# A four-layer graph network on one core: the norm ahead of the graph convolutions, done chunk by chunk in the gated-update stage, with its scaling and its split piece by piece under the first convolution

## The reference

```
h = relu((x - mean(x)) / sqrt(var(x) + 1e-5))
messages = segment_sum(h[src] @ W_msg.T + b_msg + edge_embed[type], dst)
x = x + gru_cell(messages, h, W_ih, W_hh, b_ih, b_hh)      # the gated update

h = relu((x - mean(x)) / sqrt(var(x) + 1e-5))              # the norm of this case
for k in 1, 2, 3:                                          # three graph convolutions
    h = D^-1/2 (A + I) D^-1/2 (h @ W_k.T) + b_k            # relu after the first two
x = x + h
```

## Time and profile before

| | |
|---|---|
| median of 3 runs | 6476.04 us (6473.61 to 6477.31) |
| the profiled execution, its own time | 6473.09 us |
| its span in the profile | 6471.3 us |
| TensorE busy | 4680.4 us (72%) |
| VectorE busy | 2656.4 us (41%) |
| ScalarE busy | 1449.9 us (22%) |
| GpSimd busy | 3123.8 us (48%) |
| gated-update stage | about 4600 to 5118 us of the span |
| norm block and split block | about 5120 to 5174 us |
| first, second and third convolution | begin at about 5175, 5605 and 6035 us |

### The profile page before, as it was taken

The page is one execution under the profiler, slowest core; times in us unless marked ns, Lnnn a source line. Parts: engine busy times, 40 slices in busy tenths (PEclk is TensorE's granted clock), DMA queues, the critical chain, the costliest instruction groups (busy, mean ns, idle before and its releaser), DMA issues. The chain is left out here.

```text
span 6471.3 us, 90519 instructions
## 1 busy us (share of the span) xinstructions
PE 4680.4 (72%) x25880; PEld 3137.8 (48%) x25881; DVE 2656.4 (41%) x5995; ACT 1449.9 (22%) x2542; POOL 3123.8 (48%) x3318
## 2 busy tenths in 40 slices
PE   1755555555555538888888888889599599899898
PEld 0444444444444435555555555556244344444444
DVE  4666666666666644444444444442311400000000
ACT  2111111111111123333333333331211201111000
POOL 3177777777777737777777777772000000000000
PEclk5855555555555568888888888886799799999999
DMA  3432233323323324444444444441444165555555
GB/s 98 170 93 92 93 92 93 93 92 93 93 93 93 94 79 131 134 133 132 132 131 130 130 130 130 130 130 41 140 155 158 39 218 193 168 193 193 170 193 155
DMA packets 337459, 817.56 MB, mean 126 GB/s; under 512 B 126730, under 2 KB 147748, under 8 KB 321174
## 3 DMA queue, kind: packets, MB, share of 16 engines
q1 hardware_dynamic: 218110, 516.64, 23.8%
q0 software_dynamic: 105568, 215.74, 12.2%
q10 hardware_dynamic: 13696, 84.07, 3.5%
HBM read 700.32 MB, written 114.23 MB: 126 GB/s over the span
## 5 line engine op out<-in xcount | busy, mean ns | idle before, releaser
L852 POOL DMA_INDIRECT e_rows<-scratch_table,e_staged x1616 | 1524.6, 943 | 658.1 <-issue 492.2
L1267 POOL DMA_INDIRECT e_rows<-scratch_table,e_staged x1616 | 1537.2, 951 | 587.6 <-issue 485.2
L171 PE MATMUL e_win<-e_onehot,e_rows 128*128 128x64 f32 x3232 | 783.0, 424 | 987.7 <-DMA e_rows<-scratch_table,e_staged 966.8
L171 PEld LDWEIGHTS e_win<-e_onehot,e_rows 128*128 128x128 f32 x3232 | 720.2, 328 | 1057.3 <-issue 1027.3
L1565 PE MATMUL c_sums<-ring,parts 128*128 128x512 bf16 (+1 forms) x3822 | 790.1, 368 | 80.9 <-DMA c_bias<-in_conv_b 80.9
L1375 DVE TENSOR_TENSOR e_z<-e_p,e_rows 128x512 f32<-128x512 f32 x404 | 279.3, 691 | 1155.1 <-PE e_p L1318 956.6
L1789 POOL DMA_DIRECT2D c_w<-in_convT x3 | 1.6, 535 | 1442.5 <-POOLq L77 1442.5
L1565 PEld LDWEIGHTS c_sums<-ring,parts 128*128 128x128 bf16 x3822 | 361.8, 98 | 490.1 <-DMA c_bias<-in_conv_b 81.5
L171 PEld LDWEIGHTS e_win<-e_onehot,e_msg 128*128 128x128 f32 x3232 | 477.2, 212 | 247.8 <-issue 218.0
L1298 PE MATMUL e_p<-h,we 64*128 64x512 f32 x808 | 282.8, 782 | 364.0 <-DMA h<-in_edge_T 359.9
L208 DVE TENSOR_SCALAR e_onehot<-e_iota,dst_rel,weight 128x64 f32<-128x64 f32 x1616 | 443.2, 336 | 244.7 <-issue 244.1
(11 more groups left out here) (236 smaller groups left out, 4792.2 us busy)
## 6 DMA issues: line engine op xcount, KB each, us to landing
ring<-scratch_counts SPq DMA_DIRECT2D x336, 896.0 KB, 4.7
h<-in_time_rows SPq DMA_DIRECT2D x101, 1024.0 KB
e_rows<-scratch_table,e_staged POOLq DMA_INDIRECT x3232
h<-in_edge_T SPq DMA_DIRECT2D x101, 512.0 KB, 4.2
scratch_counts<-h ACTq DMA_DIRECT2D x12, 3136.0 KB, 10.4
scratch_counts<-type_mem ACTq DMA_DIRECT2D x12, 3136.0 KB, 10.4
scratch_table<-table_tile SPq DMA_DIRECT2D x49, 512.0 KB, 2.6
ring<-scratch_counts SPq DMA_DIRECT2D x28, 224.0 KB, 2.9
```

The lines of the kernel that those rows point to most:

```text
L171: last = nc.tensor.matmul(win[:, 0:W], rows[:, j, :], onehot[:, j, :], start=(j == 0), stop=(j == J - 1))
L852: pool.indirect_dma_start(rows[:, half * NB + b, j, :], None, A["table0"], bass.IndirectOffsetOnAxis(ap=staged[:, half, b * J + j:b * J + ...
L1267: pool.indirect_dma_start(rows[:, half * NB + b, j, :], None, A["table1"], bass.IndirectOffsetOnAxis(ap=staged[:, half, b * J + j:b * J + ...
```

## The change

In the gated-update stage each chunk gets four more instructions, made right after its `x` is done. VectorE (`center`) sums the rows of the chunk, writes `x - sum/128` into `h` in one instruction, and, after ScalarE has squared it into `square`, sums the squares. ScalarE makes that square between the wait for `x` and the copy to `agg`. The block of the norm and the block of the split are gone. What is left of both now stands in the first convolution's block: `norm_pieces` on VectorE, behind its wait for weights and bias, and `split_pieces` on ScalarE. They make the variance, root, reciprocal and product with `dinv` once, and then, piece by piece, relu with scaling in one instruction, and the three parts. In product(0) of the first convolution TensorE waits for the third part of each piece before it uses it. The gated-update stage has 4 semaphores more, and each of the three convolution blocks has 7 more.

```diff
@@ -1552,7 +1552,7 @@
             pe.sem_inc(s["d_used"], 1)
             return load_flag(pe, s, pe.alloc_register(f"flag_pe_{s['used'].name}"))
 
-        def product(pe, s, above, loaded, ring, digit_ring, parts, sums, c, k, tiles, self_loops):
+        def product(pe, s, above, loaded, ring, digit_ring, parts, sums, c, k, tiles, self_loops, ready=None):
 
             width = tiles * P
 
@@ -1569,6 +1569,8 @@
             pe.wait_ge(s["out"], c + 1)
             for j in range(PIECES):
                 pe.wait_ge(loaded[j], c * 16 + 16)
+                if ready is not None:
+                    pe.wait_ge(ready, j + 1)
                 if j == PIECES - 1:
                     with pe.If(above > 0):
                         with pe.Fori(1, PLANES) as plane:
@@ -1617,7 +1619,7 @@
                 pN = psum(st, "p3N", [P, 2, BANK])
                 s = {n: sem(st, f"n3_{n}") for n in
                      ("used", "out", "w", "bias", "MT", "mh", "gates", "biased", "rz_in", "rz", "pre", "new", "v", "x", "held",
-                      "begun", "d_used", "d_loaded")}
+                      "begun", "d_used", "d_loaded", "summed", "centered", "squared", "ssq")}
                 loaded = [sem(st, f"n3_loaded{j}") for j in range(PIECES)]
                 st.callback(clear_semaphores)
                 block = st.enter_context(nc.Block())
@@ -1689,6 +1691,9 @@
                             act.wait_ge(s["pre"], u + 1)
                             nc.scalar.activation(new[:, 0:before, :], pre[:, 0:before, :], ACT.Tanh).then_inc(s["new"], 1)
                             act.wait_ge(s["x"], u + 1)
+                            act.wait_ge(s["centered"], u + 1)
+                            nc.scalar.activation(square[:, 0, 0:before, :], h[:, bass.ds(u * 4, before), :],
+                                                 ACT.Square).then_inc(s["squared"], 1)
                         if tiles:
                             act.wait_ge(s["used"], c * PIECES + 2 * PIECES)
                             nc.scalar.activation(agg[:, k, 0:tiles * P], sums[:, k, 0:tiles * P],
@@ -1708,6 +1713,19 @@
                         if tiles:
                             nc.vector.tensor_copy(held[:, k, 0:tiles, :],
                                                   h[:, bass.ds(c * 4, tiles), :]).then_inc(s["held"], 1)
+                        if before:
+                            center(c - 1, before)
+
+                    def center(u, before):
+
+                        at = bass.ds(u * 4, before)
+                        dve.wait_ge(s["x"], u + 1)
+                        nc.vector.tensor_reduce(mean[:, at], x[:, at, :], AXX, ALU.add).then_inc(s["summed"], 1)
+                        dve.wait_ge(s["summed"], u + 1)
+                        nc.vector.scalar_tensor_tensor(h[:, at, :], mean[:, at].unsqueeze(2).to_broadcast([P, before, D]),
+                                                       -1.0 / D, x[:, at, :], ALU.mult, ALU.add).then_inc(s["centered"], 1)
+                        dve.wait_ge(s["squared"], u + 1)
+                        nc.vector.tensor_reduce(ssq[:, at], square[:, 0, 0:before, :], AXX, ALU.add).then_inc(s["ssq"], 1)
 
                     def gru(u, before):
                         dve.wait_ge(s["gates"], u + 1)
@@ -1741,27 +1759,10 @@
                     run_chunks(step)(dve)
 
 
-        with ExitStack() as st:
-            s = norm_sems(st, "n4")
-            st.callback(clear_semaphores)
-            block = st.enter_context(nc.Block())
-
-            @block.vector
-            def _(dve):
-                norm_vector(dve, s, h, extra_scale=dinv)
-
-            @block.scalar
-            def _(act):
-                norm_scalar(act, s, h)
-                act.wait_ge(s["h"], PIECES)
-
-
-
         h_b = h[:, :, :].rearrange("p t d -> p (t d)").bitcast(BF16)
         parts = [[sbuf(root, f"parts3{k}", [P, NT, D], BF16)[:, :, :] for k in range(3)],
                  [v.rearrange("p (t d) -> p t d", d=D) for v in
                   (h_b[:, 0:NP], h_b[:, NP:2 * NP], type_mem[:, :].bitcast(BF16)[:, 0:NP])]]
-        split_all("split3", parts[0])
         for conv in range(3):
             last_conv = conv == 2
             with ExitStack() as st:
@@ -1779,6 +1780,11 @@
                      ("used", "out", "O", "y", "h", "part", "rest", "x", "begun",
                       "d_used", "d_loaded")}
                 loaded = [sem(st, f"c{conv}_loaded{j}") for j in range(PIECES)]
+                first_conv = conv == 0
+                s_part = [sem(st, f"c{conv}_part{k}") for k in range(3)]
+                s_gap, s_norm = [sem(st, f"c{conv}_gap{k}") for k in (1, 2)], sem(st, f"c{conv}_norm")
+                s_h0 = sem(st, f"c{conv}_h0")
+                piece_gap = sbuf(st, "piece_gap", [P, 3, PT, D]) if first_conv else None
                 s_store = sem(st, f"c{conv}_store")
                 w_base = weights_seen(32)
                 st.callback(clear_semaphores)
@@ -1807,7 +1813,8 @@
 
                     def step(c, k, tiles, before):
                         if tiles:
-                            product(pe, s, above, loaded, ring, digit_ring, now, sums, c, k, tiles, True)
+                            product(pe, s, above, loaded, ring, digit_ring, now, sums, c, k, tiles, True,
+                                    s_part[2] if first_conv and not before else None)
                         if before:
                             pe.wait_ge(s["out"], c + 2)
 
@@ -1821,6 +1828,21 @@
                 @block.scalar
                 def _(act):
                     act.sem_inc(s["out"], 2)
+
+                    def split_pieces():
+                        act.wait_ge(s_norm, 1)
+                        nc.scalar.activation(std[:, :], var[:, :], ACT.Sqrt).then_inc(s_norm, 1)
+                        for j in range(PIECES + 2):
+                            if j < PIECES:
+                                act.wait_ge(s_h0, j + 1)
+                                nc.scalar.activation(now[0][:, piece(j), :], h[:, piece(j), :], ACT.Copy).then_inc(s_part[0], 1)
+                            for k in (1, 2):
+                                if 0 <= j - k < PIECES:
+                                    act.wait_ge(s_gap[k - 1], j - k + 1)
+                                    nc.scalar.activation(now[k][:, piece(j - k), :], piece_gap[:, (j - k) % 3, :, :],
+                                                         ACT.Copy).then_inc(s_part[k], 1)
+                    if first_conv:
+                        split_pieces()
 
                     def step(c, k, tiles, before):
                         if before:
@@ -1843,6 +1865,32 @@
                 @block.vector
                 def _(dve):
                     dve.wait_ge(weights_in[0], w_base + 32)
+
+                    def norm_pieces():
+
+                        nc.vector.tensor_scalar(var[:, :], ssq[:, :], 1.0 / D, EPS, ALU.mult, ALU.add).then_inc(s_norm, 1)
+                        dve.wait_ge(s_norm, 2)
+                        nc.vector.reciprocal(rstd[:, :], std[:, :]).then_inc(s_norm, 1)
+                        dve.wait_ge(s_norm, 3)
+                        nc.vector.tensor_tensor(rstd[:, :], rstd[:, :], dinv[:, :], ALU.mult).then_inc(s_norm, 1)
+                        dve.wait_ge(s_norm, 4)
+                        for j in range(PIECES + 2):
+                            if j < PIECES:
+                                nc.vector.scalar_tensor_tensor(h[:, piece(j), :], h[:, piece(j), :], 0.0,
+                                                               rstd[:, piece(j)].unsqueeze(2).to_broadcast([P, PT, D]),
+                                                               ALU.max, ALU.mult).then_inc(s_h0, 1)
+                            if 0 <= j - 2:
+                                g = piece_gap[:, (j - 2) % 3, :, :]
+                                dve.wait_ge(s_part[1], j - 1)
+                                nc.vector.tensor_tensor(g, g, now[1][:, piece(j - 2), :], ALU.subtract).then_inc(s_gap[1], 1)
+                            if 0 <= j - 1 < PIECES:
+                                dve.wait_ge(s_part[0], j)
+                                if j >= 4:
+                                    dve.wait_ge(s_part[2], j - 3)
+                                nc.vector.tensor_tensor(piece_gap[:, (j - 1) % 3, :, :], h[:, piece(j - 1), :],
+                                                        now[0][:, piece(j - 1), :], ALU.subtract).then_inc(s_gap[0], 1)
+                    if first_conv:
+                        norm_pieces()
 
                     def step(c, k, tiles, before):
                         if not before:
```

## The result

The changed kernel takes 6443.64 us, median of 5 runs (6437.60 to 6447.53), against 6476.04 us before (6473.61 to 6478.91). The ratio is 0.9948, with a 95% interval of 0.9934 to 0.9963: faster by 0.5%, 32.4 us by the medians, where 38.0 were forecast. The forecast was 6438 with a range of 6433 to 6448. The profiled execution took 6444.22 us; its span is 6442.4, and before it was 6471.3, so that the two profiles stand 28.9 apart.

The account below looks back on a forecast made before the run. It took TensorE's 65.20 us without a matmul before the first convolution as the bound. New terms sum to 25.81, 37.98 less with 1.41 for semaphores: 6435.1, plus 2.95 to the median, 6438.1; own range 6434 to 6445, whole 6433 to 6448.

Parts of the forecast that it names:

- step of chunk 12, wait: Gated update: the short 8.37 us product gives no cover, so `agg` of chunk 11 makes TensorE 2.25 us late.
- last step, wait: Gated update's last step: the same delay of `agg`, with a `held` of one tile, adds 2.07 us.
- block change: Between gated update and first convolution: one change instead of three, 3.05 us with 29 semaphores.
- weights and bias: First convolution's start: from GpSimd's issue to TensorE's release, 7.58 us, as in the kernel before.
- root and reciprocal: First convolution's block: variance to first scaled piece, 1.26 us, its table load running under the weights' wait; upper bound 2.86.
- first piece: First convolution's block: from scaling the first piece to its third part and TensorE's release, 8.25 us.
- more semaphores: Ends of the three convolution blocks: 7 more semaphores each, 0.067 us apiece, adding 1.41 us.
- D: Rival, 0.03: TensorE stays at 1.2 GHz through the first chunk, 6468; as a stretch, first convolution matmul to the end.
- rival A: Rival, 0.09: clock falls in chunk 12's step, 7.6 us; alone, A: gated update's first product to chunk 12's short product.
- B: Rival, 0.04: TensorE not late by `agg` in the last two steps, 6434; as a stretch, the step of chunk 12.
- E: Rival, 0.02: low clock over the whole first convolution, 6820; as a stretch, gated update's first product to the end.
- C: Rival, 0.04: in the first convolution's first chunk the pieces do not overlap, 6.2 us each, giving 6443.

Follow-up runs that it names:

- e1: Changed kernel with ScalarE copying `agg` before it squares; 7486.1 us against the changed kernel's 7493.4 us, on a slower chip.
- e3: Changed kernel with TensorE waiting for all seven pieces before the first product; 7511.3 us, ratio 0.9986 to the kernel before, on a slower chip.

## Why the prediction was right, and where it was not

The mechanism was right, and nearly every term of the sum came back within 0.2 us. Forecast first, then the changed kernel's first profile:

| term | forecast | profile |
|---|---|---|
| steady chunks | 0 | 31.89 us a product, as before |
| step of chunk 12, wait | 2.25 | 2.25 |
| last step, wait | 2.07 | 2.04 (9.94 - 7.90) |
| center of chunk 12 | 1.35 | 1.37 |
| block change | 3.05 | 2.85 |
| weights and bias | 7.58 | 7.64 |
| root and reciprocal | 1.26 | 1.24 |
| first piece | 8.25 | 8.28 |
| other six pieces | 0 | 34.61 against 34.55 |
| more semaphores | 1.41 | 1.2 (D), 1.6 by the means of D |
| clock in the step of chunk 12 | 0 | 4.23 |

That the added semaphores make D longer is not shown: e1 has the same ones, and its D is 1288.5, that of the kernel before.

- **The step that failed** is rival A, "the clock falls in the step of chunk 12", to which I gave 0.09 because the new wait was "nearer to the harmless row". It came in five profiles of five with the bare wait. B grew by 6.48: 2.25 for the wait and 4.23 for matmuls at the low clock, not the full 7.6, since the clock was back after 19 of the 40 and the rest went at the high level. And the row was not harmless: the 1.17 us waits, too, are followed by a fall once in nearly every run. I had looked at one of them, and one row that kept its pace says nothing about how often the others do. The section of the Trainium skill that I had let speak for this rival ("TensorE: Matmul & The Clock Gate", "HAM oscillation — how this bites in real kernels") tells of bursts of matmuls of some 2 us that start at the half clock each time, behind waits of some 3 to 5 us. Both waits here are shorter than those, so the fall behind 2.25 us each time, and behind 1.17 us now and then, goes beyond what it states, and the measurements decide.
- **The base of the sum** was off too, by what one profile cannot show. 2.53 us in A and 2.70 at the start of the gated update (4600.41 to 4603.11) lie ahead of all that the change touches before its last steps; the second and third profile of before start it at 4601.6 and 4610.4. So 37.98 - 4.23 - 2.53 - 2.70, and 0.3 by which the other terms came out better than forecast, make the 28.9 between the two profiles. From E alone, by the means, the change gives 32.7, and 38.0 less the clock's 4.2 was 33.8.
- **In part it was luck** that 6443.64 lies within the forecast's own 6434 to 6445. That range was made of other terms, the root and the scaling above all, which did not move; the clock, which did, was counted outside it, and it cost 4.2 us of the 7.6 that were possible.
- **Rivals D and E** fell: the third window's clock is 0.94, as before. **C** fell: the chunk takes 34.61 us, and e3 prices the overlap at 16.8 us. **B** fell: both waits for `agg` are in the profile.

## What to carry to other kernels

Work that is hidden in every full turn of a loop can be open in the short last turn, as the 2.25 us were here. Look there for the copy with no slack, and put new work behind the instruction that another engine waits for, not ahead of it. When a change lengthens a wait of TensorE in front of a burst of matmuls, price the burst at the low clock as well. And when two pieces of work are moved under one cover, price the pair, since the second may be what lets the first go there.

## What the runs showed that I had not expected

- Ten useless matmuls in a 2.25 us wait saved 4.3 us behind it.
- Chips differ by 1040 us (16%) on this kernel, nearly all of it in the two stages that gather rows by indirect DMA. There GpSimd's gather took the same (943 ns in one of them), but its idle time before the 1616 gathers of that stage rose from 659.0 to 1147.3 us, and of the other from 587.7 to 1133.5. What ends the added idle time is VectorE (498.5 us at L244, 569.7 at L1375, where it was 0 and 9.8), so the gathers' own issue is not what got slower; why VectorE comes later is open. From the gated update on the changed kernel's two profiles agree within 0.7 us.
